# One instruction for both norms' variances and one for both biases, a shorter router, and undivided state slots only in two runs

## The chip, the cores and the metric

The kernel runs on one core of one Trainium2 chip. The metric is the device time of one execution in microseconds (us). TensorE (PE), VectorE (DVE), ScalarE (ACT), GpSimd (POOL) and SyncE (SP) each run their own instruction stream in order, and wait for each other through semaphores.

## The reference

One block of a network on 8 images of 192 channels and 16x16 = 256 positions (tokens):

```
x = x + conv(_ln_c(x))            # norm over channels; eps 1e-6
t = tokens(x)
t = t + ffn(_ln_t(t))             # norm over channels; eps 1e-5

conv(t): q, k = l2norm(silu(t Wq)), l2norm(silu(t Wk)); v = silu(t Wv); beta = sigmoid(t Wb)
         per head (12 heads of 16), over tokens t:
           u_t = beta_t (v_t - S^T k_t);  S = S + k_t u_t^T;  o_t = S^T q_t
         returns t + o Wo
ffn(x):  p = softmax(x router_w); top 2 of 8 experts, gates divided by their sum
         routed = sum_e gate_e * (silu(x w_gate_e) * (x w_up_e)) w_down_e
         shared = (silu(x ws_gate) * (x ws_up)) ws_down;  alpha = sigmoid(x sg_w + sg_b)
         returns alpha * shared + (1 - alpha) * routed
```

## The kernel before, in words

The 256 positions are cut into 16 chunks of 16 tokens; a chunk holds the 128 tokens of the 8 images and fills the 128 partitions. All engines go through steps c = -3 to 18 (`chunks`). In step c DVE runs the recurrence of chunk c, while the other engines and the gaps between DVE's recurrence instructions serve chunks that are earlier or later in the pipeline: `at(3, A_...)` is the first norm and the projections of chunk c+3, `at(-1, Fa_...)` the second norm and the router of chunk c-1, `Fb` the experts of chunks c-1 and c-2, `Fc` their output. The order in each step is written out by hand in each engine's `step`.

The recurrence of one chunk is 64 **slots** on DVE, four for each token: slot 4i multiplies the state by k (L1363, `Pr`), 4i+1 sums (L1365, `u`), 4i+2 forms k u^T (L1367, `bank`), 4i+3 adds it to the state (L1371, `SH`). Each needs the result of the one before. A slot is either **divided** (two instructions of half the heads, 96 elements each, so that one half works while the other's result lands) or **whole** (one instruction of 192), if its number is in `WHOLE`. `others(slot)` puts the small work of the other chunks behind a slot: `at(32, -1, Fa_var)` stands behind slot 32. A whole slot has to wait for its predecessor's result, and small work behind the predecessor fills that time.

Around the change:
- First norm (chunk c+3): `A_stats`, `A_mean` (L1091, L1095) make mean and variance, `A_var` (L1101) adds eps into `ve[:,0]`, POOL's `rsqrt` (L922) raises `ve` to -1/2 into `rs` for both norms at once, `A_bias` (L1108) makes `nmr1` = -mean*rstd, and ACT's `A_h`, `A_xh` use it. Second norm (chunk c-1): `Fa_stats`, `Fa_mean` (L1112, L1116), `Fa_var` (L1122), the same `rsqrt`, `Fa_bias` (L1128), then ACT's `Fa_h` (L662) writes `h2`, PE turns it, ACT's `Fa_hT` (L670) copies `hiT`, DVE's `Fa_split` (L1134) makes `loT`, and PE multiplies it by the router and the experts (L436 to L440).
- POOL, after `rsqrt`, does `hidden` 7, the products of state and q of half 0 of chunk c (L933), three `hidden`, the sums (L940, L957), and, after three small operations on k and q and two `hidden`, the same for half 1. DVE's `Fa_otok` (L1197) behind slot 23 of the next step waits for the second L957.
- ACT, after `Fa_h`, goes through some expert units, loads the table for exp and ln, does `A_inv` and `Fa_exp` (L678, L679: exp of the logits and of minus the shared gate's), loads the silu table, and copies `hidT` (`hidden` 2, L717). PE waits for that copy before `Fb_turn` 3 (L448), which stands ahead of `Fb_down` 2 (L463) and `fill(1, 0)` (L403). A `fill` broadcasts k for two tokens into PSUM, and slot 0 of the next step waits for `fill(1, 0)`.
- Router on DVE: `G_dif` makes the 64 differences of 8 logits, `G_eq` and `G_gt` compare them (equal ones count by order, table `lower`), `G_rank` sums to a rank, `G_sel` takes exp where rank < 2; `G_den`, `G_recip`, `G_rest`, `G_coef`, `G_gate` make the gates.

## Time and profile before

| | |
|---|---|
| time, median of 3 runs | 483.62 us (483.32 to 485.1) |
| the profiled execution's own time | 484.68 us |
| its span, first to last instruction | 482.9 us |
| granted clock of TensorE | 1.00 |
| DVE, PE, POOL, ACT busy | 86%, 86%, 85%, 72% of the span |
| DVE busy in each 25 us between 85 and 435 us | 24.3 to 24.9 us |

An engine's row in a timeline has its start, the time from its first start to its last end, and what it did; rows with x2 are two instructions of one form. The time from one row's start to the next row's start is what an instruction holds back its engine; this is less than its duration where two overlap.

### The profile page before, as it was taken

To read this page: it belongs to the slowest core of one execution; us is meant where nothing else is said; L and a number is where in the kernel's file an instruction comes from. 1 tells how busy PE (TensorE), PEld (TensorE's weight loads), DVE (VectorE), ACT (ScalarE), POOL (GpSimd) and SP (SyncE) were. 2 spreads that over 40 slices of the span, in tenths; PEclk is the share of its full clock that TensorE was granted. 3 is DMA by queue.
4 is the path that set the end of the run, shared out by engine and by line. 5 is a ranking of instruction groups with operands and counts; after the bars stand their busy time and mean duration, and the time that the engine had idled before them with its cause. 6 is when DMAs were issued, how large, how long until landed. Compare 5 with 4: busy or idle time off the path is not lost.

```text
span 482.9 us, 10362 instructions
## 1 busy us (share of the span) xinstructions
PE 416.3 (86%) x2400; PEld 384.6 (80%) x2400; DVE 415.3 (86%) x2258; ACT 347.4 (72%) x1003; POOL 410.8 (85%) x525
## 2 busy tenths in 40 slices
PE   1445265999999999999999999999999989899996
PEld 0323144898998999999999999999999979799895
DVE  4259899999999999999999999999999999996200
ACT  3699466587878687787878696969696847475862
POOL 4479798999999999999999999999999999986340
PEclk9999999999999999999999999999999999999999
DMA  6658372633233323323232233323232332300301
GB/s 163 164 131 176 92 194 76 124 88 117 78 83 80 88 65 96 76 87 87 71 87 83 87 87 83 93 80 92 72 99 71 84 90 76 94 5 1 115 2 16
DMA packets 43437, 42.91 MB, mean 89 GB/s; under 512 B 20144, under 2 KB 35184, under 8 KB 43376
## 3 DMA queue, kind: packets, MB, share of 16 engines
q1 hardware_dynamic: 42768, 42.05, 32.8%
q8 instruction: 19, 0.31, 0.3%
q14 instruction: 42, 0.34, 0.2%
q10 hardware_dynamic: 608, 0.21, 0.2%
HBM read 35.95 MB, written 6.29 MB: 87 GB/s over the span
## 4 chain that ended last, share of the span: by engine, by line
DVE 58%; PE 15%; POOL 9%; issue 8%; SPq 5%; DMA 3%; ACT 2%; POOLq 0%; ACTq 0%; DVEq 0%
DVE Pr L1363 13%; DVE bank L1367 13%; DVE u L1365 12%; DVE SH L1371 10%; PE bank L463 3%; POOL PQ L940 3%; POOL PQ L933 2%; POOL hid L978 2%; PE bank L436 1%; DMA k_scratch<-khl 1%; SPq L278 1%; PE bank L448 1%; PE bank L440 1%; PE bank L439 1%; PE bank L438 1%
## 5 line engine op out<-in xcount | busy, mean ns | idle before, releaser
L978 POOL TENSOR_TENSOR hid<-sg,ug 128x192 f32<-128x192 f32 x192 | 112.7, 606 | 22.0 <-ACT ug L707 18.8
L933 POOL TENSOR_TENSOR PQ<-SH,QB 128x768 f32<-128x768 f32 x62 | 112.6, 1838 | 0.7 <-DVE SH L1371 0.7
L706 ACT ACTIVATE sg<-bank 128x192 f32<-128x192 f32 x192 | 64.4, 336 | 61.1 <-PE bank L440 48.2
L940 POOL TENSOR_TENSOR PQ<-PQ 128x768 f32<-128x768 f32 (+2 forms) x93 | 102.9, 1106 | 6.1
L463 PE MATMUL bank<-Wd,hidT 128*128 128x192 f32 x576 | 106.6, 326 | 0.0
L1367 DVE TENSOR_TENSOR bank<-bank,u 128x96 f32<-128x96 f32 (+1 forms) x467 | 104.7, 266 | 0.6
L1363 DVE TENSOR_TENSOR Pr<-SH,bank 128x96 f32<-128x96 f32 (+1 forms) x437 | 101.3, 266 | 3.3 <-PE bank L403 1.3
L1365 DVE TENSOR_REDUCE u<-Pr 128x6 f32<-128x102 f32 (+1 forms) x437 | 102.6, 269 | 0.4
L1371 DVE TENSOR_TENSOR SH<-SH,bank 128x96 f32<-128x96 f32 (+1 forms) x467 | 102.2, 257 | 0.3
L463 PEld LDWEIGHTS bank<-Wd,hidT 128*128 128x128 f32 x576 | 94.5, 190 | 0.0
L436 PE MATMUL bank<-Whi,hiT 128*128 128x384 f32 (+1 forms) x192 | 73.1, 381 | 1.1 <-DVE loT L1134 1.1
L403 PE MATMUL bank<-KR,Sel 128*128 128x384 f32 x128 | 54.2, 426 | 18.7 <-DVE SH L1371 12.6
L440 PE MATMUL bank<-W,loT 128*128 128x384 f32 (+1 forms) x192 | 66.1, 344 | 0.0
L439 PE MATMUL bank<-W,hiT 128*128 128x384 f32 (+1 forms) x192 | 65.9, 343 | 0.0
L438 PE MATMUL bank<-Whi,loT 128*128 128x384 f32 (+1 forms) x192 | 65.9, 343 | 0.0
L437 PE MATMUL bank<-Wlo,hiT 128*128 128x384 f32 (+1 forms) x192 | 65.7, 342 | 0.0
L707 ACT ACTIVATE ug<-bank,gate 128x192 f32<-128x192 f32 x128 | 53.6, 419 | 0.0
L448 PE MATMUL bank<-ident,hid 128*128 128x128 f32 x288 | 45.6, 276 | 8.7 <-ACT hidT L717 8.0
L741 ACT ACT_TABLE_LOAD x38 | 48.8, 1283 | 0.7
L717 ACT ACTIVATE hidT<-bank 128x512 f32<-128x512 f32 (+1 forms) x80 | 45.7, 572 | 2.2 <-PE bank L448 2.0
L448 PEld LDWEIGHTS bank<-ident,hid 128*128 128x128 f32 x288 | 33.9, 141 | 14.7 <-issue 11.5
L403 PEld LDWEIGHTS bank<-KR,Sel 128*128 128x128 f32 x128 | 26.1, 206 | 23.1 <-DVE SH L1371 12.4
(141 smaller groups left out, 815.9 us busy)
## 6 DMA issues: line engine op xcount, KB each, us to landing
QB<-q_scratch SPq DMA_DIRECT2D x64, 384.0 KB
k_scratch<-khl SPq DMA_DIRECT2D x64, 48.0 KB, 1.7
KR<-k_scratch SPq DMA_DIRECT2D x32, 96.0 KB, 2.4
q_scratch<-qn SPq DMA_DIRECT2D x64, 24.0 KB, 1.6
...
```

What stands on the lines that cost most here:

```text
L403: mm(bKB[f % 2][:, 0:2 * BR * G], Sel[:, f].rearrange("p b x e -> p (b x e)"), KR[:, p, :], start=True, stop=True).then_inc(s_fill, 1)
L436: mm(to, hiT[:, p, 0:P], Whi0[:, w], start=True, stop=False)
L440: mm(to, loT[:, p, P:2 * P], W1[:, w], start=False, stop=True).then_inc(s_up, 1)
L448: last = tr(bHt[:, (k - lo) * P:(k - lo + 1) * P], hid[:, k % (KT // 2) * P:(k % (KT // 2) + 1) * P], ident[:, :])
L463: last = mm(bDn[:, 0:C], hidT[:, turn_half(g), k - lo, :], Wd[:, k, :], start=False, stop=(k == KT - 1))
L933: tt(PQ[:, at * BR * HP:(at + n) * BR * HP].rearrange("p (i b h) d -> p i b (h d)", i=n, b=BR), SH[:, lo:lo + n].rearrange("p i b h d -> p ...
L940: chained(tt(PQ[:, :, 0:w], PQ[:, :, 0:w], PQ[:, :, w:2 * w], ALU.add))
L978: tt(hid[:, r * H:(r + 1) * H], sg[:, m % RING], ug[:, m % RING], ALU.mult).then_inc(s_hid, 1)
L1363: v = each(slot, lambda lo, hi: count(tt(Pr[:, lo:hi, i, :, 0:D], prev[:, lo:hi], KB[:, lo:hi], ALU.mult)), Sb)
L1365: v = each(slot + 1, lambda lo, hi: count(nc.vector.tensor_reduce(u[:, i % 2, lo:hi], Pr[:, lo:hi, i], X, ALU.add, negate=True)), v)
L1367: v = each(slot + 2, lambda lo, hi: count(tt(KB[:, lo:hi], KB[:, lo:hi], u[:, i % 2, lo:hi].unsqueeze(3).to_broadcast([P, hi - lo, HP, D]) ...
L1371: ins = tt(SH[:, i, lo:hi], prev[:, lo:hi], KB[:, lo:hi], ALU.add)
```

## The change

`var_both` adds both eps values to both variances in one instruction behind slot 34 (before: two, behind slot 32), and `bias_both` makes both biases in one behind slot 38 (before: the second norm's behind slot 36, the first norm's behind 52). `Fa_mean` moves from slot 32 to 33, `A_vT` from 37 to 35. The router compares once, difference >= `above`: this table holds 0 where an equal logit counts and the smallest normal number where it doesn't. And the gates come from sel times 1/den times 1/(1 + exp(+sgate)), for which ACT does a third, one-column exp. `WHOLE` goes from 16 slots to 8: 31 to 34, 44, 48 to 50. In steps 13 to 15, where no first norm is left, `Fa_var` and `Fa_bias` stand at the new places.

```diff
-WHOLE = frozenset((9, 31, 32, 37, 44, 48, 49, 50, 51, 52, 53, 54, 55, 56, 57, 58))
+WHOLE = frozenset((31, 32, 33, 34, 44, 48, 49, 50))
+BOTH = NC - 4
+TINY = 1.1754944e-38
...
+        def variance2(q):
+            return (s_ve1, q + 5) if q < BOTH else (s_ve2, q - BOTH + 1)
+        def bias2(q):
+            return (s_nm1, q + 5) if q < BOTH else (s_nm2, q - BOTH + 1)
...
             def Fa_x1(q, p):
-                act.wait_ge(s_ve2, q + 1)
+                act.wait_ge(*variance2(q))
...
             def Fa_h(q, p):
-                act.wait_ge(s_nm2, q + 1)
+                act.wait_ge(*bias2(q))
...
                 f(prob[:, 0:E], bUp[0][:, 0:E], ACT.Exp, bias=negmax[:, 0:1])
-                f(prob[:, E:E + 1], bUp[0][:, E:E + 1], ACT.Exp, scale=-1.0, bias=neg_sgb[:, 0:1]).then_inc(s_pr, 1)
+                f(prob[:, E:E + 1], bUp[0][:, E:E + 1], ACT.Exp, scale=-1.0, bias=neg_sgb[:, 0:1])
+                f(prob[:, E + 1:E + 2], bUp[0][:, E:E + 1], ACT.Exp, bias=sgb[:, 0:1]).then_inc(s_pr, 1)
...
+            def var_both(q, p):
+                dve.wait_ge(*w["mv1"])
+                dve.wait_ge(*w["mv2"])
+                dve.wait_ge(s_rs, q + 4)
+                tt(ve[:, :], mv[:, :, 1], eps[:, :], ALU.add).then_inc(s_ve1, 1)
+
+            def bias_both(q, p):
+                dve.wait_ge(s_rs, q + 5)
+                dve.wait_ge(s_h, q + 4)
+                dve.wait_ge(s_xh, q + 4)
+                if later(q, 1):
+                    dve.wait_ge(s_h2, q)
+                nc.vector.scalar_tensor_tensor(out=nmr[:, :], in0=mv[:, :, 0], scalar=-1.0, in1=rs[:, :], op0=ALU.mult,
+                                               op1=ALU.mult).then_inc(s_nm1, 1)
...
-            def G_eq(q, p, slot):
-            def G_gt(q, p, slot):
+            def G_above(q, p, slot):
                 dve.wait_ge(s_nmx, q + 1)
+                w["above"] = count(tt(table(slot, 0), table(slot, 0), above[:, :, :], ALU.is_ge))
...
-                w["one"] = count(ts(den[:, 1:2], prob[:, E:E + 1], 1.0, None, ALU.add))
+                w["one"] = count(ts(den[:, 1:3], prob[:, E:E + 2], 1.0, None, ALU.add))
...
-            def G_rest(q, p, slot):
-            def G_coef(q, p, slot):
             def G_gate(q, p, slot):
-                dve.wait_ge(*w["co"])
-                tt(gate[:, p], scratch(slot, 0, 1).to_broadcast([P, E]), sel[:, :], ALU.mult).then_inc(s_gate, 1)
+                dve.wait_ge(*w["rden"])
+                ts(gate[:, p], sel[:, :], rden[:, p, 0:1], rden[:, p, 2:3], ALU.mult, ALU.mult).then_inc(s_gate, 1)
...
                         at(32, -1, Fa_stats)
-                        at(32, -1, Fa_mean)
-                        at(32, 3, A_var)
-                        at(32, -1, Fa_var)
-                        at(36, -1, Fa_bias)
-                        at(37, 1, A_vT)
+                        at(33, -1, Fa_mean)
+                        at(34, -1, var_both if c + 3 < NC else Fa_var)
+                        at(35, 1, A_vT)
+                        at(38, -1, bias_both if c + 3 < NC else Fa_bias)
...
-                        at(49, -1, G_eq, done)
-                        at(50, -1, G_gt, done)
-                        at(51, -1, G_rank, done)
-                        at(52, 3, A_bias)
+                        at(49, -1, G_above, done)
+                        at(50, -1, G_rank, done)
                         at(53, -1, G_sel, done)
                         at(54, -1, G_den, done)
-                        at(55, -1, G_recip, done)
-                        at(56, -1, G_rest, done)
-                        at(57, -1, G_coef, done)
+                        at(56, -1, G_recip, done)
                         at(58, -1, G_gate, done)
```

What DVE does before the change from slot 32 to slot 37 of a middle step (`st`, `mv` are the norms' statistics, `Pr`, `u`, `bank`, `SH` the slots; `128x6x16 x2` or `128x96 x2` is a divided slot):

```order
L1363 TENSOR_TENSOR Pr<-SH,bank 128x2x6x16
L1112 BN_STATS st<-bank 128x6
L1116 BN_AGGR mv<-st 128x2
L1101 TENSOR_SCALAR ve<-mv 128x1
L1122 TENSOR_SCALAR ve<-mv 128x1
L1365 TENSOR_REDUCE u<-Pr 128x6 x2
L1367 TENSOR_TENSOR bank<-bank,u 128x96 x2
L1371 TENSOR_TENSOR SH<-SH,bank 128x96 x2
L1363 TENSOR_TENSOR Pr<-SH,bank 128x6x16 x2
L1128 TENSOR_SCALAR nmr<-mv,rs 128x1
L1365 TENSOR_REDUCE u<-Pr 128x12
L1172 STREAM_TRANSPOSE vT<-vn 128x192
```

And after the change, from slot 32 to slot 38 of the same step:

```order
L1369 TENSOR_TENSOR Pr<-SH,bank 128x2x6x16
L1125 BN_STATS st<-bank 128x6
L1371 TENSOR_REDUCE u<-Pr 128x12
L1129 BN_AGGR mv<-st 128x2
L1373 TENSOR_TENSOR bank<-bank,u 128x2x96
L1147 TENSOR_TENSOR ve<-mv,eps 128x2
L1377 TENSOR_TENSOR SH<-SH,bank 128x96 x2
L1200 STREAM_TRANSPOSE vT<-vn 128x192
L1369 TENSOR_TENSOR Pr<-SH,bank 128x6x16 x2
L1371 TENSOR_REDUCE u<-Pr 128x6 x2
L1373 TENSOR_TENSOR bank<-bank,u 128x96 x2
L1155 SCALAR_TENSOR_TENSOR nmr<-mv,rs 128x2
```

Between the second norm's statistics and `ve` two whole slots now stand, and between `ve` and `nmr` four slots and the transpose, where there were four slots.

What DVE does after the change from slot 50 to slot 58 (before, each of these slots was whole, and had one or two small operations behind it):

```order
L1373 TENSOR_TENSOR bank<-bank,u 128x2x96
L1251 TENSOR_REDUCE bank<-bank 128x8
L1377 TENSOR_TENSOR SH<-SH,bank 128x96 x2
L1369 TENSOR_TENSOR Pr<-SH,bank 128x6x16 x2
L1371 TENSOR_REDUCE u<-Pr 128x6 x2
L1257 SCALAR_TENSOR_TENSOR sel<-bank,prob 128x8
L1259 TENSOR_SCALAR den<-prob 128x2
L1373 TENSOR_TENSOR bank<-bank,u 128x96 x2
L1263 TENSOR_REDUCE den<-sel 128x1
L1377 TENSOR_TENSOR SH<-SH,bank 128x96 x2
L1369 TENSOR_TENSOR Pr<-SH,bank 128x6x16 x2
L1269 RECIPROCAL rden<-den 128x3
```

Slots 51 to 58 are now divided, and the small operations stand further apart.

## Rows read from the trace of the kernel before

**Rows 1.** The page: busy time of the engines, and shares of the chain.
```profile
PE 416.3 (86%) x2400; PEld 384.6 (80%) x2400; DVE 415.3 (86%) x2258; ACT 347.4 (72%) x1003; POOL 410.8 (85%) x525
...
DVE 58%; PE 15%; POOL 9%; issue 8%; SPq 5%; DMA 3%; ACT 2%; POOLq 0%; ACTq 0%; DVEq 0%
```

**Rows 2.** Waits from 160 to 360 us: who waits for whom, total, times, longest.
```profile
PE bank L448 <- ACT hidT L717: 5.2, 8, 0.7
POOL rs L922 <- DVE ve L1122: 4.0, 8, 0.7
...
DVE ve L1122 <- DVE mv L1116: 0.3, 1, 0.3
```

**Rows 3.** Timeline of DVE, the instruction behind slot 23 in four steps.
```profile
92.14 0.38 DVE L1197 STREAM_TRANSPOSE otok<-oT 128x192 f32<-128x192 f32 x1
...
243.81 0.37 DVE L1197 STREAM_TRANSPOSE otok<-oT 128x192 f32<-128x192 f32 x1
...
269.01 0.37 DVE L1197 STREAM_TRANSPOSE otok<-oT 128x192 f32<-128x192 f32 x1
...
345.10 0.38 DVE L1197 STREAM_TRANSPOSE otok<-oT 128x192 f32<-128x192 f32 x1
```

**Rows 4.** Timeline of DVE, slots 32 to 38 of one step.
```profile
247.13 0.36 DVE L1363 TENSOR_TENSOR Pr<-SH,bank 128x192 f32<-128x192 f32 x1
247.40 0.36 DVE L1112 BATCH_NORM_STATS2 st<-bank 128x6 f32<-128x192 f32 x1
247.80 0.18 DVE L1116 BATCH_NORM_AGGREGATE mv<-st 128x2 f32<-128x6 f32 x1
...
248.01 0.15 DVE L1122 TENSOR_SCALAR ve<-mv 128x1 f32<-128x1 f32 x1
248.09 0.42 DVE L1365 TENSOR_REDUCE u<-Pr 128x6 f32<-128x102 f32 x2
...
249.40 0.21 DVE L1128 TENSOR_SCALAR nmr<-mv,rs 128x1 f32<-128x1 f32 x1
...
249.87 0.37 DVE L1172 STREAM_TRANSPOSE vT<-vn 128x192 f32<-128x192 f32 x1
250.16 0.40 DVE L1367 TENSOR_TENSOR bank<-bank,u 128x96 f32<-128x96 f32 x2
```

**Rows 5.** Timeline of DVE, slots 48 and 59 of the same step.
```profile
254.40 0.36 DVE L1363 TENSOR_TENSOR Pr<-SH,bank 128x192 f32<-128x192 f32 x1
254.67 0.23 DVE L1214 TENSOR_TENSOR bank<-bank,logit 128x64 f32<-128x64 f32 x1
...
258.84 0.42 DVE L1371 TENSOR_TENSOR SH<-SH,bank 128x96 f32<-128x96 f32 x2
```

**Rows 6.** Timeline of POOL, the same step.
```profile
248.43 0.70 POOL L922 TENSOR_TENSOR rs<-ve,neg_half 128x2 f32<-128x2 f32 x1 [0.40 <-DVE ve L1122]
...
268.51 0.37 POOL L957 TENSOR_TENSOR oT<-PQ 128x96 f32<-128x96 f32 x1
```

**Rows 7.** Timeline of ACT, the same step.
```profile
250.00 0.47 ACT L662 ACTIVATE h<-bank,nmr,rs 128x128 f32<-128x128 f32 x1
...
255.77 0.25 ACT L678 ACTIVATE prob<-bank,negmax 128x8 f32<-128x8 f32 x1
255.92 0.25 ACT L679 ACTIVATE prob<-bank,neg_sgb 128x1 f32<-128x1 f32 x1
...
257.48 0.60 ACT L717 ACTIVATE hidT<-bank 128x512 f32<-128x512 f32 x1
```

**Rows 8.** Timeline of PE, this step and the next.
```profile
258.23 0.63 PE L448 MATMUL bank<-ident,hid 128*128 128x128 f32 x4 [0.69 <-ACT hidT L717]
...
259.86 0.47 PE L403 MATMUL bank<-KR,Sel 128*128 128x384 f32 x1
...
283.45 0.63 PE L448 MATMUL bank<-ident,hid 128*128 128x128 f32 x4 [0.62 <-ACT hidT L717]
```

**Rows 9.** Timeline of DVE, slot 0 of the next step.
```profile
260.55 0.42 DVE L1363 TENSOR_TENSOR Pr<-SH,bank 128x96 f32<-128x96 f32 x2
```

More of the change, by code:

```diff
@@ L78, in build @@
         neg_half, eps6, one = sb("neg_half", [P, 2]), sb("eps6", [P, 1]), sb("one", [P, 1])
+        eps = sb("eps", [P, 2])
         sgb, neg_sgb = sb("sgb", [P, 1]), sb("neg_sgb", [P, 1])
-        lower = sb("lower", [P, E, E])
+        above = sb("above", [P, E, E])
         xs0, xs = sb("xs0", [C0, NB, T]), sb("xs1", [P, NB, T])
         xs1 = xs[C1:P]
-        st1, mv1 = sb("st1", [P, 6]), sb("mv1", [P, 2])
-        ve, rs, nmr1 = sb("ve", [P, 2]), sb("rs", [P, 2]), sb("nmr1", [P, 1])
+        st1, mv = sb("st1", [P, 6]), sb("mv", [P, 2, 2])
+        mv1, mv2 = mv[:, 0], mv[:, 1]
+        ve, rs, nmr = sb("ve", [P, 2]), sb("rs", [P, 2]), sb("nmr", [P, 2])
+        nmr1, nmr2 = nmr[:, 0:1], nmr[:, 1:2]
         rstd1, rstd2 = rs[:, 0:1], rs[:, 1:2]
@@ L863, in _ @@
             act.wait_ge(s_x[0], 32)
-            act.wait_ge(s_const, 4)
+            act.wait_ge(s_const, 6)
             chunks(step)
@@ L1063, in _ @@
                                pattern=[[-1, P]], channel_multiplier=1).then_inc(s_id, 1)
-            for t, val in ((neg_half, -0.5), (eps6, 1e-6), (one, 1.0), (ve, 1.0)):
+            for t, val in ((neg_half, -0.5), (eps6, 1e-6), (one, 1.0), (ve, 1.0), (eps[:, 0:1], 1e-6), (eps[:, 1:2], 1e-5)):
                 pool.memset(t[:, :], val).then_inc(s_const, 1)
-            pool.memset(lower[:, :, :], 1.0).then_inc(s_low, 1)
+            pool.memset(above[:, :, :], TINY).then_inc(s_low, 1)
             pool.wait_ge(s_low, 1)
-            pool.affine_select(out=lower[:, :, :], in_=lower[:, :, :], compare_op=ALU.is_gt, fill=0.0, base=0,
-                               pattern=[[1, E], [-1, E]], channel_multiplier=0).then_inc(s_low, 1)
+            pool.affine_select(out=above[:, :, :], in_=above[:, :, :], compare_op=ALU.is_ge, fill=0.0, base=0,
+                               pattern=[[-1, E], [1, E]], channel_multiplier=0).then_inc(s_low, 1)
             pool.memset(SH[:, T - 1], 0.0).then_inc(s_zero, 1)
@@ L1074, in _ @@
                 pool.memset(b, 0.0).then_inc(s_clear, 1)
-            pool.wait_ge(s_const, 4)
+            pool.wait_ge(s_const, 6)
             chunks(step)
@@ L1215, in G_dif @@
                    ALU.subtract).then_inc(s_nmx, 1)
-            def G_eq(q, p, slot):
+            def G_above(q, p, slot):
                 dve.wait_ge(s_nmx, q + 1)
-                w["eq"] = count(nc.vector.scalar_tensor_tensor(out=eq[:, :, :], in0=table(slot, 0), scalar=0.0,
-                                                               in1=lower[:, :, :], op0=ALU.is_equal, op1=ALU.mult))
-            def G_gt(q, p, slot):
-                dve.wait_ge(*w["eq"])
-                w["gt"] = count(nc.vector.scalar_tensor_tensor(out=table(slot, 0), in0=table(slot, 0), scalar=0.0,
-                                                               in1=eq[:, :, :], op0=ALU.is_gt, op1=ALU.add))
+                w["above"] = count(tt(table(slot, 0), table(slot, 0), above[:, :, :], ALU.is_ge))
             def G_rank(q, p, slot):
-                dve.wait_ge(*w["gt"])
+                dve.wait_ge(*w["above"])
                 w["rank"] = count(nc.vector.tensor_reduce(scratch(slot, E * E, E), table(slot, 0), X, ALU.add))
@@ L1247, in G_recip, with G_gate @@
                 w["rden"] = count(nc.vector.reciprocal(rden[:, p], den[:, :]))
-            def G_rest(q, p, slot):
+            def G_gate(q, p, slot):
                 dve.wait_ge(*w["rden"])
-                w["om"] = count(ts(coef[:, :], rden[:, p, 1:2], -1.0, 1.0, ALU.mult, ALU.add))
-            def G_coef(q, p, slot):
-                dve.wait_ge(*w["om"])
-                w["co"] = count(ts(scratch(slot, 0, 1), coef[:, :], rden[:, p, 0:1], None, ALU.mult))
-            def G_gate(q, p, slot):
-                dve.wait_ge(*w["co"])
-                tt(gate[:, p], scratch(slot, 0, 1).to_broadcast([P, E]), sel[:, :], ALU.mult).then_inc(s_gate, 1)
+                ts(gate[:, p], sel[:, :], rden[:, p, 0:1], rden[:, p, 2:3], ALU.mult, ALU.mult).then_inc(s_gate, 1)
             def negate_sgb():
@@ L1320, in others @@
                         at(48, -1, G_dif, done)
-                        at(49, -1, G_eq, done)
-                        at(50, -1, G_gt, done)
-                        at(51, -1, G_rank, done)
+                        at(49, -1, G_above, done)
+                        at(50, -1, G_rank, done)
                         at(53, -1, G_sel, done)
@@ L1326, in others @@
                         at(55, -1, G_recip, done)
-                        at(56, -1, G_rest, done)
-                        at(57, -1, G_coef, done)
                         at(58, -1, G_gate, done)
@@ L1377, in step @@
                         others(slot + 3)
-            dve.wait_ge(s_const, 4)
+            dve.wait_ge(s_const, 6)
             dve.wait_ge(s_low, 2)
```

13 lines of the change are left out of this document (6 added, 7 removed).

## The prediction

> **What bounds the kernel now.** The page says that four engines are busy for 72 to 86% of the span, and the chain that ended last lies on DVE for 58% [rows 1]. In the table of waits from 160 to 360 us, eight steps, the reader is to see that DVE waits once, for 0.3 us, while POOL waits for DVE's variance in each step and PE for ACT's `hidT` in each [rows 2]. So DVE sets the pace, by its own instructions: from `otok` to `otok` one undisturbed step takes 269.01 - 243.81 = 25.20 us, and over ten steps (92.14 to 345.10) the mean is 25.30, so that about 0.1 us a step goes to pauses like that 0.3 [rows 3]. A saving on DVE counts only as far as the loops through the other engines are shorter than 25.20. I therefore read the timelines for three loops.
>
> *The POOL loop.* `ve` is done at 248.01 + 0.15 = 248.16, `rsqrt` starts at 248.43 [rows 4, 6], and POOL works without a gap to the end of the second L957 at 268.88: 20.45 us [rows 6]. `otok` starts at 269.01, 0.13 later [rows 3]. A DVE instruction that really waits for a result starts 0.04 after it (247.40 + 0.36 to 247.80) [rows 4], so only 0.09 of this is slack. From `otok` (243.81) DVE needs 4.35 to `ve`. The loop's own length: 0.27 + 20.45 + 0.04 + 4.35 = 25.11.
>
> *The ACT-PE-DVE loop.* `nmr` ends at 249.61, ACT's `h` starts at 250.00 [rows 4, 7]: 0.39, so 0.35 of slack. ACT then goes on without a wait to `hidT` at 257.48, PE waits for it and resumes at 258.23, `fill(1, 0)` ends at 260.33, and slot 0 starts at 260.55: 0.22, so 0.18 of slack [rows 7, 8, 9]. Then DVE's slots 0 to 36 lead to the next `nmr`. Own length: 25.20 - 0.53 = 24.67.
>
> *The PE-ACT loop*, without DVE: PE resumes behind `hidT` at 258.23 and at 283.45, 25.22 apart [rows 8]. PE lacks nothing else in between, and ACT waits for PE's expert units, so this loop is full already.
>
> **The change, part by part.**
>
> *DVE's own time.* A divided slot costs 0.33: from slot 33 to `nmr` four of them take 249.40 - 248.09 = 1.31 [rows 4]. A whole one with a small operation behind it costs 0.40: eleven take 258.84 - 254.40 = 4.44 [rows 5]. Slots 48 to 58 are now three whole and eight divided ones, 1.21 + 2.64, and five small operations behind divided slots. Each costs about 0.09 there (such a one holds the queue for 248.09 - 248.01 = 0.08 [rows 4], the gate with two pointer operands perhaps 0.12): 0.45. Sum 4.30, saving 0.14. Around slot 32, from `st` to the start of slot 35: before 248.09 - 247.40 = 0.69 and two divided slots 0.66, together 1.35. After: `st` 0.27 (what a whole instruction holds the queue, 247.40 - 247.13), then two whole slots 0.80, with `mv` and `ve` inside: 1.07. Saving 0.28, of which about 0.05 is given back by the longer list of semaphores of `bias_both`. Slot 9 divided: 0.07 less. In all 0.4 to 0.44: DVE alone would need 24.8 us a step. The second comparison, the two gate operations and the two small norm operations are gone in this sum.
>
> *A page against this.* The Trainium skill, page "VectorE: DVE Perf Modes", section on the TRN2 errata, says that every instruction pays a fixed latency that shows between instructions, so many small tiles are worse than a large one, and gives (N + 151)/0.96 ns for fp32: 257 for 96 elements, 357 for 192. The durations agree (0.25 and 0.36), but by that rule a divided slot would cost 0.51, and here its halves overlap and it costs 0.33. It is kept as a rival below.
>
> *What is moved.* `ve` was ready 0.76 after `st` began (247.40 to 248.16). Now it is `st` 0.27, slot 33 whole until slot 34 may start 0.40, slot 34 until the small operation 0.27, and 0.15: 1.09. So **`ve` comes 0.33 later** against slot 30. From `ve`'s start to `nmr`'s it was 249.40 - 248.01 = 1.39. Now: the rest of slot 34 0.13, slot 35 0.33, `vT` 0.29 (249.87 to 250.16), slots 36 to 38 0.99: 1.74, or 0.35 more. So **`nmr` comes 0.68 later**. The first norm's bias comes much earlier than at slot 52, which serves nobody: ACT stands elsewhere in its order. Queued behind `rsqrt` on POOL are products, sums and then the L957 that `otok` waits for. Queued behind `Fa_h` on ACT are the units, `hiT`, the table loads, `hidT`.
>
> *What is added.* One more exp on ACT, between the second exp and the table load, in the gapless stretch from `h` to `hidT`. Bounds: 0, if something hid it, and its duration of 0.25. I take 0.15, from one exp's start to the next (255.77 to 255.92) [rows 7]. The Trainium skill, page "ScalarE: Activation LUTs", rules for kernel authors, budgets about 0.3 us for an activation. With that in place of 0.15, the two loops through ACT would be 0.15 longer.
>
> *The loops after.* POOL: 25.11 + 0.33 = **25.44**. ACT-PE-DVE: 24.67 + 0.68 + 0.15 - 0.07 = **25.43**. PE-ACT: 25.22 + 0.15 = **25.37**. All are longer than DVE's 24.8 and than the 25.20 of before. DVE has to stand still for about 0.65 us a step: at `otok` for POOL, at `loT` and slot 0 for ACT and PE. The two longest run side by side, so they don't add up.
>
> **Sum.** Steps 2 to 12, eleven of them, 25.44 - 25.20: +2.65. DVE's pauses of 0.1 a step now partly fall into its new idle time; between all and nothing of 11 x 0.1 I take half: -0.5. First step, where PE and ACT are still held up by the weights: the later `nmr` costs 0 to 0.7, taken 0.35. Steps 13 to 15 have no first norm, so shorter loops and more that DVE saves (bounds per step -0.4, its own saving, and +0.25, as above): taken 0. Behind the last step ACT's table, exp, table stands alone ahead of PE's wait, so the extra exp shows once more: +0.15. Together +2.65: 482.9 becomes a span of about 485.5, and the profiled execution's 484.68 about 487.3. That execution was 1.1 above the median of the three runs, and I put the difference on the median: 483.62 + 2.65 = 486.3.
>
> **Rivals.**
> 1. *Only the PE-ACT loop binds*, because the POOL loop and the ACT-PE-DVE loop have slack that I don't see (a shorter reaction of `rsqrt`, 0.27 now, with one semaphore less in its list). For it: the loops differ by 0.07 only. Against: both gaps are read directly. 11 x (25.37 - 25.30) + 0.15 = +0.9: 484.5.
> 2. *The exp is hidden and the moved operations too*: the floor is PE's present 25.22. 11 x (25.22 - 25.30), and up to 0.4 each in the last three steps: -2.1 at most, -1.2 in the middle: 482.4.
> 3. *DVE's saving comes through in full*: 14 steps of 0.4 and the pauses as before: 478. This needs POOL's 20.45 us to shrink by 0.65, which decides it: from 25.44 down to 25.30 nothing is won, and only below it the sign turns. For it: POOL's operations might run faster while DVE is idle. Against: POOL has no gap in that stretch.
> 4. *The waits hit in turn, not side by side*: `otok` late one time, then slot 0 late, with PE's and ACT's phases pushed by each; 0.5 to 0.6 a step instead of 0.25. 11 x 0.55, less what the pauses give: +5.8: 489.4.
> 5. *Each instruction pays in full*: halves that don't overlap, 0.50 instead of 0.36 for eight slots, 1.1 a step, +16 over 15 steps: 500. Forty-eight slots of every step are divided already and run at 0.33. This is the rule of the Trainium skill's VectorE page above; the trace does not agree with it.
>
> **How the numbers follow.** Forecast 0.50 (by itself 485.2 to 487.8), rival 1 0.19, rival 2 0.11, rival 3 0.09, rival 4 0.10, rival 5 0.01. A measurement here tells about 0.5%, 2.4 us, from no change: 481.2 to 486.0. The forecast's range lies across the upper edge, some three fifths above it: 0.30 slower, 0.20 same. With rivals 4 and 5 slower is 0.41. Rival 1 and most of rival 2 are same: 0.20 + 0.19 + 0.09 = 0.48. Rival 3 and the low end of 2 are faster: 0.09 + 0.02 = 0.11. Range: from 482.0, which leaves out rival 3 and a part of 2, to 488.8, which leaves out most of rival 4.
>
> **What the profile after would show.** Right: from `otok` to `otok` 25.4 to 25.5 in a middle step; DVE's waits with new lines of some tenths a step, `otok` for POOL's `oT`, `loT` for ACT's `hiT` or slot 0 for PE's L403 (now with new line numbers); POOL's idle time ahead of `rsqrt` about 0.65 where it was 0.40; ACT's `h` right behind `nmr`; DVE with 2,306 instructions (12 steps with 8 more and 5 fewer, three with 8 more and 3 fewer, the tail with 3 fewer), ACT with 1,019. Wrong: `otok` to `otok` of 24.8 with no wait on DVE (rival 3); 25.22 or 25.37 with `otok` not waiting (rivals 2, 1). The step most open to error is that a gap of 0.1 us, read at 0.01, decides between winning and losing.

## The result, and the profile after

The changed kernel takes 505.70 us (median of 4 runs, 505.62 to 506.04), the kernel before 483.51 us (4 runs, 483.32 to 485.1). The ratio is 1.0435 (95% interval 1.0411 to 1.046): 4.35% slower, some 22 us, where the prediction had 2.65. A few single executions further down came out far above the others of their kernel (553.98 us in e4, 504.24 in e9, 842.56 in e13); the ratios leave them out, the medians in the tables hold them.

The page of the kernel after: span, busy time, and the chain that ended last by engine and by line.
```profile
span 503.9 us, 10387 instructions
...
PE 416.7 (83%) x2400; PEld 382.8 (76%) x2400; DVE 430.9 (86%) x2306; ACT 351.8 (70%) x1019; POOL 413.1 (82%) x527
...
DVE 46%; PE 15%; ACT 14%; issue 8%; POOL 8%; SPq 5%; DMA 3%; ACTq 0%; POOLq 0%; DVEq 0%
DVE Pr L1369 10%; DVE u L1371 9%; DVE bank L1373 8%; DVE SH L1377 7%; ACT L754 5%; PE bank L475 4%; DVE nmr L1155 4%; POOL PQ L953 3%; PE bank L460 2%; ACT hidT L730 2%; POOL PQ L946 2%; POOL hid L991 2%; SPq L290 1%; DMA k_scratch<-khl 1%; ACT h L675 1%
```

DVE's share is what it was [rows 1], but its busy time has grown by 15.6 us, though the change was to relieve it. In the last line stands a name that did not appear in the prediction's sum: `nmr` L1155, the merged bias, with 4% of the span. Nothing else on DVE got longer by much; the groups of DVE instructions, each form apart (busy us, mean ns | idle time before), give the size:
```profile
L1155 DVE SCALAR_TENSOR_TENSOR nmr<-mv,rs 128x2 f32<-128x2 f32 x12 | 19.3, 1610 | 0.2 <-issue 0.2
...
L1274 DVE TENSOR_SCALAR gate<-sel,rden 128x8 f32<-128x8 f32 x16 | 5.1, 318 | 0.0
L1259 DVE TENSOR_SCALAR den<-prob 128x2 f32<-128x2 f32 x16 | 3.8, 239 | 0.0
...
L1147 DVE TENSOR_TENSOR ve<-mv,eps 128x2 f32<-128x2 f32 x12 | 1.8, 150 | 0.0
```

Twelve instructions on two elements a partition take 1.61 us each on average, where the old bias on one element took 0.21 [rows 4]. The merged variance beside it, as small, takes 0.15. The timelines of DVE and of POOL in one step show what the long one has for company (start, us from first start to last end):
```profile
260.79 0.42 DVE L1373 TENSOR_TENSOR bank<-bank,u 128x96 f32<-128x96 f32 x2
261.12 1.76 DVE L1155 SCALAR_TENSOR_TENSOR nmr<-mv,rs 128x2 f32<-128x2 f32 x1
262.81 0.41 DVE L1377 TENSOR_TENSOR SH<-SH,bank 128x96 f32<-128x96 f32 x2
```
```profile
259.82 0.70 POOL L935 TENSOR_TENSOR rs<-ve,neg_half 128x2 f32<-128x2 f32 x1 [0.87 <-DVE ve L1147]
260.49 0.60 POOL L991 TENSOR_TENSOR hid<-sg,ug 128x192 f32<-128x192 f32 x1
261.04 1.83 POOL L946 TENSOR_TENSOR PQ<-SH,QB 128x768 f32<-128x768 f32 x1
```

Two ends are to be compared here: `nmr` ends at 261.12 + 1.76 = 262.88, and POOL's product, which started 0.08 before it, at 261.04 + 1.83 = 262.87. DVE's next instruction starts 1.69 after `nmr` did; a small operation here holds it for about 0.1. The product reads two tensors in SBUF; so does `nmr` (`mv` and `rs`), and of all small operations that DVE has in a step, only this one and `ve` do. One view of this line over the whole execution (duration ns min/median/max, then who waited for it):
```profile
L1155 DVE SCALAR_TENSOR_TENSOR nmr<-mv,rs x12: 288/1758/1762, 72.3 to 369.8; 128x2 f32<-128x2 f32 x12
...
  ACT h L674: 19.9, 12
```

The waits from 160 to 360 us, seven steps (total, times, longest), answer to [rows 2]:
```profile
ACT h L674 <- DVE nmr L1155: 11.3, 7, 1.6
...
PE bank L367 <- ACT h L675: 10.1, 7, 1.4
...
ACT oc L663 <- PE bank L363: 9.2, 7, 1.3
PE bank L460 <- ACT hidT L730: 7.5, 8, 0.9
...
POOL rs L935 <- DVE ve L1147: 6.1, 7, 0.9
...
DVE loT L1162 <- ACT hiT L682: 3.2, 7, 0.5
```

ACT waits 1.6 us a step for the bias, PE for ACT's `h` behind it, and the wait `DVE loT`, which the prediction named, is there with 0.46 a step. The step follows from the twelve starts of `otok` over which both norms run, eleven steps apart (first and last start stand in the row behind the three durations); it answers to [rows 3]:
```profile
L1225 DVE STREAM_TRANSPOSE otok<-oT x12: 367/371/373, 92.3 to 390.3; 128x192 f32<-128x192 f32 x12
```
(390.3 - 92.3)/11 = 27.09 us a step; in the kernel before it is 25.30 [rows 3]. 11 x 1.79 = 19.7 of the span's 21.0 us are in these eleven steps.

Three theories stood to be told apart. **Port:** a DVE instruction with two tensor inputs in SBUF waits until POOL's running instruction ends. **Form:** the merged instruction is slow in itself, by its operation, its two elements or its four semaphores. **Places:** the later places of variance and bias and the third exp make the longer step, as my prediction had it, only more so.

### The profile page after: what moved, and what is told of

It is laid out like the page before. It is cut to its first block, busy times and chain, and to the rows that moved or that the text cites. A ratio compares the mean times of both kernels' runs of the same rounds, so it can differ in the third digit from the quotient of the medians.

```text
span 503.9 us, 10387 instructions
## 1 busy us (share of the span) xinstructions
PE 416.7 (83%) x2400; PEld 382.8 (76%) x2400; DVE 430.9 (86%) x2306; ACT 351.8 (70%) x1019; POOL 413.1 (82%) x527
## 4 chain that ended last, share of the span: by engine, by line
DVE 46%; PE 15%; ACT 14%; issue 8%; POOL 8%; SPq 5%; DMA 3%; ACTq 0%; POOLq 0%; DVEq 0%
DVE Pr L1369 10%; DVE u L1371 9%; DVE bank L1373 8%; DVE SH L1377 7%; ACT L754 5%; PE bank L475 4%; DVE nmr L1155 4%; POOL PQ L953 3%; PE bank L460 2%; ACT hidT L730 2%; POOL PQ L946 2%; POOL hid L991 2%; SPq L290 1%; DMA k_scratch<-khl 1%; ACT h L675 1%
## 5 line engine op out<-in xcount | busy, mean ns | idle before, releaser
L991 POOL TENSOR_TENSOR hid<-sg,ug 128x192 f32<-128x192 f32 x192 | 113.9, 612 | 35.6 <-ACT ug L720 29.0
L953 POOL TENSOR_TENSOR PQ<-PQ 128x768 f32<-128x768 f32 (+2 forms) x93 | 103.1, 1109 | 6.1
L1369 DVE TENSOR_TENSOR Pr<-SH,bank 128x96 f32<-128x96 f32 (+1 forms) x467 | 102.5, 257 | 3.1 <-PE bank L415 1.1
L1371 DVE TENSOR_REDUCE u<-Pr 128x6 f32<-128x102 f32 (+1 forms) x482 | 104.2, 255 | 0.1
L1377 DVE TENSOR_TENSOR SH<-SH,bank 128x96 f32<-128x96 f32 (+1 forms) x497 | 103.7, 248 | 0.3
```

Source lines behind the costliest of these rows:

```text
L953: chained(tt(PQ[:, :, 0:w], PQ[:, :, 0:w], PQ[:, :, w:2 * w], ALU.add))
L991: tt(hid[:, r * H:(r + 1) * H], sg[:, m % RING], ug[:, m % RING], ALU.mult).then_inc(s_hid, 1)
L1369: v = each(slot, lambda lo, hi: count(tt(Pr[:, lo:hi, i, :, 0:D], prev[:, lo:hi], KB[:, lo:hi], ALU.mult)), Sb)
L1371: v = each(slot + 1, lambda lo, hi: count(nc.vector.tensor_reduce(u[:, i % 2, lo:hi], Pr[:, lo:hi, i], X, ALU.add, negate=True)), v)
L1377: ins = tt(SH[:, i, lo:hi], prev[:, lo:hi], KB[:, lo:hi], ALU.add)
```

## The experiments

The kernels of one group ran on the same chip beside the kernel before, and ratios are to that (its medians: 484.13, 484.41, 484.56 and 484.12 us in the four groups). A mean step is worked out as above, over the same eleven steps, from the one execution of each kernel that was profiled.

### First group: is it the port, the form or the places?

**e1_two_biases**
```diff
-                nc.vector.scalar_tensor_tensor(out=nmr[:, :], in0=mv[:, :, 0], scalar=-1.0, in1=rs[:, :], op0=ALU.mult,
-                                               op1=ALU.mult).then_inc(s_nm1, 1)
+                ts(nmr2[:, :], mv2[:, 0:1], rstd2, -1.0, ALU.mult, ALU.mult)
+                ts(nmr1[:, :], mv1[:, 0:1], rstd1, -1.0, ALU.mult, ALU.mult).then_inc(s_nm1, 1)
```


> The changed kernel with its one merged bias instruction (two tensor inputs in SBUF) written as the two old instructions of one tensor input and a pointer each, at the same slot 38 and behind the same waits; all else as changed. Port theory (a DVE instruction with two tensor inputs in SBUF waits until GpSimd's running instruction ends): each bias takes 0.21 us and holds DVE about 0.12, so DVE gets back 1.69 - 0.24 = 1.45 us a step; the step falls from 27.10 to between 25.2 and 25.5, and the time from 505.7 to 482-488. Rival, the later places of variance and bias and the third exp make the step: the step stays near 27.1 and the time near 505.

**e2_slot37**
```diff
-                        at(38, -1, bias_both if c + 3 < NC else Fa_bias)
+                        at(37, -1, bias_both if c + 3 < NC else Fa_bias)
```


> The changed kernel with the merged bias instruction unchanged in form, but one slot earlier (37 for 38). Port theory: it starts near the end of GpSimd's 0.6 us instruction hid, before the product of 1.83 us; it takes 0.3 to 0.4 us, holds DVE about 0.3, and the time is 486-490. Rival, the instruction of this form and shape is slow in itself, or its list of semaphores is: it still takes 1.6 to 1.8 us and the time stays at 503-506.

**e4_lone_two_sbuf** (the kernel before, with)
```diff
...
+            def extra(q, p):
+                nc.vector.scalar_tensor_tensor(out=junk[:, :], in0=neg_half[:, :], scalar=-1.0, in1=neg_half[:, :], op0=ALU.mult,
+                                               op1=ALU.mult)
...
+                        if c + 3 < NC:
+                            at(38, -1, extra)
```


> The kernel before with one instruction added in 12 steps, at slot 38: a scalar_tensor_tensor of 2 elements a partition whose two tensor inputs are one constant in SBUF and which nobody waits for. It has no semaphore. In this kernel GpSimd's first product (1.84 us) ends about 1.0 us after slot 38. Port theory: each takes 0.9 to 1.1 us and holds DVE nearly as long, +10 to +12 us, time 493 to 496. Rival, the form is slow by itself: 1.6 to 1.8 us each, about 502. Rival, it waited in the changed kernel for its data or its list of semaphores: 0.16 us each, 484 to 485.

**e5_lone_psum**: the same with `in1=bKB[0][:, 0:2]`, which is in PSUM.

> The kernel before with the same lone instruction at the same slot in 12 steps, but with its second tensor input in PSUM. Port theory: 0.16 us each and the time 483.5 to 485.5. Rival, the form is slow in itself: as with both inputs in SBUF, 1 us or more each and 493 or more.

Measured:

| | ratio (95%) | median us | mean step | the instruction in question |
|---|---|---|---|---|
| e1 | 1.0138 (1.0109 to 1.0167) | 490.83 | 25.72 | 0.20 us each |
| e2 | 1.0103 (1.0069 to 1.0136) | 488.82 | 25.43 | 0.31 us |
| e4 | 1.0231 (1.0192 to 1.0269) | 495.91 | 26.18 | 1.04 us |
| e5 | 0.9997 (0.9979 to 1.0014) | 483.98 | 25.29 | 0.14 us |

The same merged instruction with the same operands and semaphores is short one slot earlier. DVE and POOL in e2_slot37:
```profile
250.75 0.30 DVE L1155 SCALAR_TENSOR_TENSOR nmr<-mv,rs 128x2 f32<-128x2 f32 x1
```
```profile
250.44 0.60 POOL L991 TENSOR_TENSOR hid<-sg,ug 128x192 f32<-128x192 f32 x1
251.00 1.83 POOL L946 TENSOR_TENSOR PQ<-SH,QB 128x768 f32<-128x768 f32 x1
```
It ends at 251.05, with `hid` at 251.04, not with the product that follows. And an instruction that nobody waits for, on a constant, behind no semaphore, put into the kernel before, lasts until POOL's product there ends, to 0.02 us (255.83 + 1.04 = 256.87; 255.01 + 1.84 = 256.85); e4_lone_two_sbuf, DVE and POOL:
```profile
255.83 1.04 DVE L1132 SCALAR_TENSOR_TENSOR junk<-neg_half 128x2 f32<-128x2 f32 x1
256.79 0.41 DVE L1378 TENSOR_TENSOR SH<-SH,bank 128x96 f32<-128x96 f32 x2
```
```profile
255.01 1.84 POOL L934 TENSOR_TENSOR PQ<-SH,QB 128x768 f32<-128x768 f32 x1
```
With one of its inputs in PSUM it is an ordinary small operation (view of the line in e5_lone_psum, ns min/median/max):
```profile
L1132 DVE SCALAR_TENSOR_TENSOR junk<-neg_half,bank x12: 141/144/148, 71.9 to 350.6; 128x2 f32<-128x2 f32 x12
```
So the port theory stands, and form and semaphores are out: with two inputs in SBUF the same form takes 0.31, 1.04 and 1.76 us, each time what POOL leaves of its own instruction, and with one of them in PSUM 0.14. In e4 each of them costs 0.96 us of DVE's queue, and its step is 26.18 - 25.29 = 0.89 longer than e5's; the ratio, from three executions, gives 0.0231 x 484 = 11.2 us (9.3 to 13.0) for the twelve: where DVE sets the pace, such a wait is paid nearly in full. Places are out as the main cause: e1 keeps them all, and with it 4.35% have become 1.38%.

The Trainium skill says this, page "SBUF — State Buffer", section "Who interferes with whom": a VectorE instruction with two SBUF inputs contends with a GpSimd instruction that reads SBUF, since its second input comes through a read interface that the two share, and the one that comes second is blocked until the other's instruction ends. The trace agrees: POOL's instructions in these rows all read SBUF, and DVE's end 0.01 to 0.02 us after them.

The kernel before had a row for it already, the other way round. At its end DVE takes over one product with two inputs in SBUF, and POOL's `hid`, which needs 1.15 for two, takes 3.06 (before, DVE and POOL):
```profile
436.51 1.76 DVE L1180 TENSOR_TENSOR PQ<-SH,QB 128x1536 f32<-128x1536 f32 x1
```
```profile
435.10 1.15 POOL L978 TENSOR_TENSOR hid<-sg,ug 128x192 f32<-128x192 f32 x2
436.93 3.06 POOL L978 TENSOR_TENSOR hid<-sg,ug 128x192 f32<-128x192 f32 x2 [0.69 <-ACT ug L707]
```
The first of the two takes 1.79 and ends 0.45 after DVE's product (436.51 + 1.76 = 438.27).

What e1 and e2 did not bring back, 1.0 to 1.4%, is more than the 0.55% of the prediction, and e1 missed the 482 to 488 expected of it. In both, the router's new forms have become long in places (view of the two lines in e2_slot37; in the kernel after their medians are 159 and 282 ns):
```profile
L1259 DVE TENSOR_SCALAR den<-prob x16: 160/487/916, 79.7 to 457.2; 128x2 f32<-128x2 f32 x16
L1274 DVE TENSOR_SCALAR gate<-sel,rden x16: 293/381/530, 81.8 to 457.8; 128x8 f32<-128x8 f32 x16
```
What they cost in e2 is open: its step of 25.43 is that of e9 below (25.44), where they are short. In e1, ACT's `h` waits for the second of the two biases and starts 6.69 after `otok`, against 6.49 in e3 below (251.59 - 244.90, 252.55 - 246.06), and its usual step is 25.65 for e3's 25.49; one step of 26.86, in which `den` takes 0.85 and `gate` 0.62, comes on top.

### Second group: the same without any such wait

**e3_psum_means**: means and variances are written to PSUM, so that the merged bias has one input there.
```diff
...
+            mvp = scratch(33, 96, 4).rearrange("p (n k) -> p n k", n=2)
+            def means_both(q, p):
+                dve.wait_ge(*w["st1"])
+                nc.vector.bn_aggr(mvp[:, 0], st1[:, :]).then_inc(s_chain, 1)
...
+                w["mvp"] = count(nc.vector.bn_aggr(mvp[:, 1], st2[:, :]))
...
-                nc.vector.scalar_tensor_tensor(out=nmr[:, :], in0=mv[:, :, 0], scalar=-1.0, in1=rs[:, :], op0=ALU.mult,
+                nc.vector.scalar_tensor_tensor(out=nmr[:, :], in0=mvp[:, :, 0], scalar=-1.0, in1=rs[:, :], op0=ALU.mult,
...
-                        at(31, 3, A_mean)
...
-                        at(33, -1, Fa_mean)
+                        at(33, -1, means_both if c + 3 < NC else Fa_mean)
```


> The changed kernel with the means and variances of both norms written to PSUM (both of them at slot 33), so that the merged bias instruction, of the same form and size, at the same slot 38 and behind the same semaphores, reads one tensor in PSUM and one in SBUF. Port theory: it takes 0.15 to 0.2 us where it took 1.76, the step falls from 27.10 to about 25.45, and the time is 485-489. Rival, merging the two biases is slow in any form: 1.6 us or more each and 503-506.

**e7_no_port**: e3, with the router's selection, denominators and gate input in PSUM too, and
```diff
...
-                w["one"] = count(ts(den[:, 1:3], prob[:, E:E + 2], 1.0, None, ALU.add))
+                w["one"] = count(ts(scratch(53, 81, 2), prob[:, E:E + 2], 1.0, None, ALU.add))
...
-                ts(gate[:, p], sel[:, :], rden[:, p, 0:1], rden[:, p, 2:3], ALU.mult, ALU.mult).then_inc(s_gate, 1)
+                ts(gate[:, p], scratch(53, 72, 8), rden[:, p, 0:1], rden[:, p, 2:3], ALU.mult, ALU.mult).then_inc(s_gate, 1)
...
-                        at(56, -1, G_recip, done)
-                        at(58, -1, G_gate, done)
+                        at(54, -1, G_recip, done)
+                        at(54, -1, G_gate, done)
```


> As the last one, and the router's selection and denominators in PSUM too (reciprocal and gate moved to slot 54, where that bank is still free), so that no small instruction of VectorE reads two tensors in SBUF or runs from SBUF to SBUF over an even number of elements, but the two variances' sum. Port theory: den takes 0.16 and gate 0.28 us in every step, none ends 25 ns after an instruction of GpSimd; DVE gets back the 0.07 to 0.35 us a step that both waited; step 25.1 to 25.4, time 481-487. Rival, the loop over GpSimd and the late bias sets the step, as my prediction had it: it stays at 25.4 to 25.45 however little DVE does, time 486-488, with DVE idle for the difference.

**e8_norms_old**: the changed kernel with the old norms.
```diff
...
-                        at(33, -1, Fa_mean)
-                        at(34, -1, var_both if c + 3 < NC else Fa_var)
-                        at(35, 1, A_vT)
-                        at(38, -1, bias_both if c + 3 < NC else Fa_bias)
+                        at(32, -1, Fa_mean)
+                        at(32, 3, A_var)
+                        at(32, -1, Fa_var)
+                        at(36, -1, Fa_bias)
+                        at(37, 1, A_vT)
...
+                        at(52, 3, A_bias)
```


> The router's and the undivided slots' part of the change alone: variances and biases as in the kernel before, four instructions at the old slots. DVE's own time is some 0.2 us a step under that of before, less what den (two elements) and gate (SBUF to SBUF) wait for GpSimd, 0 to 0.45 us. Port theory: the time is that of before within 1%, and den or gate end 25 ns after an instruction of GpSimd wherever they are long. Rival, the third exp or the router's new order costs by itself: over 488 with den and gate short.

**e9_no_port_37**: e7 with `bias_both` at slot 37.

> As e7_no_port, with the merged bias one slot earlier (37). If the late bias held loT (VectorE idle 0.4 us a step before it with the bias at 38 in two instructions, 0.0 with it at 37), the step is that of VectorE's own work, 24.8 to 25.1, and the time 478-483, under the kernel before. Rival, the loops over GpSimd's rsqrt and the expert stream set it: 25.4, 486-488.

| | ratio (95%) | median us | mean step | `nmr` | `den` min/median/max ns | `gate` |
|---|---|---|---|---|---|---|
| e3 | 1.0073 (1.005 to 1.0096) | 488.53 | 25.49 | 0.15 us | 158/306/596 | median 383 |
| e7 | 1.0066 (1.0042 to 1.009) | 488.21 | 25.53 | 0.15 | 151/152/155 | 284/285/286 |
| e8 | 1.007 (1.0047 to 1.0093) | 488.49 | 25.59 | 0.21 | 157/160/939 | 282/284/633 |
| e9 | 1.0067 (1.0039 to 1.0094) | 488.43 | 25.44 | 0.15 | as e7 | as e7 |

e3 is the changed kernel but for where its means lie. Its `nmr`, over all twelve:
```profile
L1163 DVE SCALAR_TENSOR_TENSOR nmr<-bank,rs x12: 148/150/160, 73.3 to 354.6; 128x2 f32<-128x2 f32 x12
```
From 1.0435 to 1.0073: 3.6 of the 4.35% were the second SBUF input of twelve instructions of two elements, 17.5 us. Their busy time gives the same: 19.3 in the kernel after, less 12 x 0.15.

e8 shows the second, smaller form of the same thing. DVE in a step of 26.44 us, and POOL beside it:
```profile
182.52 0.89 DVE L1259 TENSOR_SCALAR den<-prob 128x2 f32<-128x2 f32 x1
183.32 0.42 DVE L1375 TENSOR_TENSOR bank<-bank,u 128x96 f32<-128x96 f32 x2
...
185.13 0.63 DVE L1274 TENSOR_SCALAR gate<-sel,rden 128x8 f32<-128x8 f32 x1
```
```profile
180.52 2.87 POOL L953 TENSOR_TENSOR PQ<-PQ 128x768 f32<-128x768 f32 x2
...
185.14 0.59 POOL L991 TENSOR_TENSOR hid<-sg,ug 128x192 f32<-128x192 f32 x1
```
`den` has one tensor input, two elements, from SBUF to SBUF; it ends at 183.41, POOL's L953 at 183.39. `gate` ends at 185.76, POOL's `hid` at 185.73. Where they meet nothing they take 0.16 and 0.28. With one element, in the kernel before, `den` was never long (142/143/144 ns over its 16), and with their input or output in PSUM (e7) both are constant to 4 ns. Most steps of e8 without such a meeting take 25.25 us, the three with both 26.44. That is 3 x 1.19 = 3.6 us, about the whole of its 0.7%. The Trainium skill, page "VectorE: DVE Perf Modes", section "Mode 2×_2P — use both read ports for one tensor", has a rule for it: an fp32 tensor_scalar from SBUF to SBUF whose outermost dimension is even in source and destination reads through both interfaces, and PSUM on either side excludes that. The runs agree.

e7 and e9 are then the changed kernel with every such wait gone, and they test the sum that I had made. In e7, as in e3, with the bias at the predicted slot 38, DVE pauses only ahead of `loT`, which starts 0.87 after the slot before it where an unpaused one has 0.33; `otok` doesn't wait. In e9 a step takes 25.44, and DVE stands idle at just the two places named: at `otok`, and at `loT` (waits of DVE and POOL from 160 to 360 us, e9_no_port_37):
```profile
POOL rs L935 <- DVE ve L1146: 5.2, 8, 0.7
...
DVE loT L1170 <- ACT hiT L682: 1.4, 7, 0.2
```
and DVE's and POOL's rows at `otok`: it starts 0.53 after the divided slot before it, which holds the queue for 0.32 or 0.33, and 0.03 after POOL's `oT` ended (244.74 + 0.37 = 245.11).
```profile
244.61 0.41 DVE L1384 TENSOR_TENSOR SH<-SH,bank 128x96 f32<-128x96 f32 x2
245.14 0.38 DVE L1233 STREAM_TRANSPOSE otok<-oT 128x192 f32<-128x192 f32 x1
```
```profile
241.17 3.49 POOL L953 TENSOR_TENSOR PQ<-PQ 128x768 f32<-128x768 f32 x3
244.74 0.37 POOL L970 TENSOR_TENSOR oT<-PQ 128x96 f32<-128x96 f32 x1
```
That is the POOL loop of the prediction, at its length of 25.44. By starts, DVE pauses 0.2 at `otok` and 0.27 ahead of `loT` (0.60 for 0.33), a little more than the view of waits has.

### Third group: the places, the exp, the merging alone

**e10_early**: e7 with the old places (the variances, which wait for both means, at 33).
```diff
                         at(32, -1, Fa_stats)
-                        at(33, -1, means_both if c + 3 < NC else Fa_mean)
-                        at(34, -1, var_both if c + 3 < NC else Fa_var)
-                        at(35, 1, A_vT)
-                        at(38, -1, bias_both if c + 3 < NC else Fa_bias)
+                        at(32, -1, means_both if c + 3 < NC else Fa_mean)
+                        at(33, -1, var_both if c + 3 < NC else Fa_var)
+                        at(36, -1, bias_both if c + 3 < NC else Fa_bias)
+                        at(37, 1, A_vT)
```


> As e7_no_port, but with means, variances and bias at the slots of the kernel before (32, 33 and 36 for 33, 34 and 38). With no wait for GpSimd left, the step was 25.50 us with the bias at 38 and 25.43 at 37, and VectorE stood idle 0.2 us before loT and 0.22 us in slot 32. Loop theory (the late variance and the late bias of my prediction hold the step at 25.4): with both back the step falls to VectorE's own work, 24.9 to 25.2, and the time to 479-484. Rival, the third exp and the expert stream set it: 25.4 and 486-489.

**e12_late_places**: the kernel before with
```diff
-                        at(32, -1, Fa_mean)
-                        at(32, 3, A_var)
-                        at(32, -1, Fa_var)
-                        at(36, -1, Fa_bias)
-                        at(37, 1, A_vT)
+                        at(33, -1, Fa_mean)
+                        at(34, 3, A_var)
+                        at(34, -1, Fa_var)
+                        at(35, 1, A_vT)
+                        at(38, -1, Fa_bias)
```


> The kernel before with its old instructions, but the norms' mean, variances, transpose vT and bias at the places of the changed kernel (33, 34, 35 and 38 for 32, 32, 37 and 36). Loop theory: 25.40 to 25.45 a step for 25.18, that is 486-487. Rival, VectorE alone sets the pace of before and the places are free: 25.2 and 483-485.

**e6_extra_exp**: the kernel before with
```diff
...
-                f(prob[:, E:E + 1], bUp[0][:, E:E + 1], ACT.Exp, scale=-1.0, bias=neg_sgb[:, 0:1]).then_inc(s_pr, 1)
+                f(prob[:, E:E + 1], bUp[0][:, E:E + 1], ACT.Exp, scale=-1.0, bias=neg_sgb[:, 0:1])
+                f(prob[:, E + 1:E + 2], bUp[0][:, E:E + 1], ACT.Exp, bias=sgb[:, 0:1]).then_inc(s_pr, 1)
```


> The kernel before with the third exp added on ScalarE behind the second, its result read by nobody. My prediction's loop over VectorE and the expert stream: +0.15 us of VectorE waiting before sel, of which all is on the path: 25.33 a step, 485.5-486.5. Rival, it is hidden: VectorE comes to sel later than ScalarE ends, 483.5-484.5.

**e11_norms_psum**: the kernel before with `means_both`, `var_both` and `bias_both` as in e10 and
```diff
-WHOLE = frozenset((9, 31, 32, 37, 44, 48, 49, 50, 51, 52, 53, 54, 55, 56, 57, 58))
+WHOLE = frozenset((9, 32, 37, 44, 48, 49, 50, 51, 53, 54, 55, 56, 57, 58))
```


> The kernel before with only the norms merged, means and variances in PSUM, at the old places (statistics and means 32, variances 33, bias 36), router and exps as before, slots 31 and 52 divided. If the merging itself is worth what it takes from VectorE (four small instructions fewer by two, two slots divided), 0.2 to 0.3 us a step: 24.9 to 25.05 and 479-482. Rival, another loop holds the step where it is: 25.18 and 483-485, with VectorE idle for the difference.

| | ratio (95%) | median us | mean step |
|---|---|---|---|
| e10 | 1.0 (0.9984 to 1.0016) | 484.7 | 25.35 |
| e12 | 1.0169 (1.0145 to 1.0194) | 492.65 | 25.84 |
| e6 | 1.0021 (1.0004 to 1.0038) | 485.45 | 25.35 |
| e11 | 1.0066 (1.004 to 1.0093) | 487.88 | 25.44 |

e10 against e7: the places alone, with all else of the change, are worth 0.66%, give or take 0.3. With them back and no wait for POOL, the change costs and brings nothing: 1.0, where both expectations were off (I had 479 to 484 or 486 to 489). e12 shows the same from the other side, and harder than I had expected: 0.53 us a step and not 0.25, DVE waiting for `hiT`:
```profile
DVE loT L1134 <- ACT hiT L670: 2.8, 6, 0.5
```
(Waits of DVE from 160 to 320 us.) With the old instructions and the old `WHOLE`, the second norm's bias starts 6.55 us after `otok` there, in e3 6.25, and the undisturbed step is longer by about as much, 25.76 for 25.49.

The third exp costs 0.2%, 1.0 us. The expectation for e6 had 2, from a full 0.15 in each step; the prediction's rival 1 had 0.9, since only what exceeds DVE's pace counts. PE shows it plainly (e6_extra_exp, two resumptions behind `hidT`, one step apart):
```profile
235.24 0.63 PE L448 MATMUL bank<-ident,hid 128*128 128x128 f32 x4 [0.82 <-ACT hidT L718]
...
260.59 0.63 PE L448 MATMUL bank<-ident,hid 128*128 128x128 f32 x4 [0.83 <-ACT hidT L718]
```
From 159 to 337 us all seven such intervals are 25.35 to 25.38, while DVE's steps go from 25.18 to 25.85. In the kernel before, five of eight are 25.22 or 25.23 [rows 8], the other three 25.36 to 25.38. So with the third exp the loop between PE and ACT is about 25.36 long, as the prediction had it (25.37).

e11 is a miss: it has less work on DVE than the kernel before and the old places, and is 0.7% slower. No wait of DVE on another engine over 0.3 us shows between 160 and 320. Part of the cause is in its `WHOLE`: slots 31 and 52, which are divided and stand ahead of a whole slot with nothing behind them, hold DVE for 0.54 and 0.51 in each step, where the whole slot with its small operation held it for 0.47 and 0.38. That is 0.20 a step more, as much as the whole edit was to save at the least. One step of 27.98 near the end is in no other trace; the profiled execution is the slowest of e11's ten (490.97, the fastest 485.59), and I have no cause for that step.

### Fourth group: can the saving on DVE be had?

**e13_between**: e7 with
```diff
-                        at(34, -1, var_both if c + 3 < NC else Fa_var)
+                        at(33, -1, var_both if c + 3 < NC else Fa_var)
                         at(35, 1, A_vT)
-                        at(38, -1, bias_both if c + 3 < NC else Fa_bias)
+                        at(36, -1, bias_both if c + 3 < NC else Fa_bias)
```


> As e9_no_port_37, but with the variances' sum at slot 33 right behind the means and the bias at 36. Loop theory: the loops over GpSimd's rsqrt and over ScalarE's h shorten by the slot, 0.3 us, to 25.1; VectorE's own work is 24.9 to 25.1; step 25.0 to 25.2 and the time 480-483.5, under the kernel before or level. Rival, saving and lateness are one thing (what the late places hide on VectorE is what comes back as stalls when they are early): 25.25 to 25.4 and 484-486.

**e14_between_den53**: e13 with `at(53, -1, G_den, done)` for 54.

> As e13_between, with den's sum at slot 53 in place of 54, so that two and not three instructions that wait for each other stand in slot 54. If VectorE sets the step there, 0.05 to 0.1 us a step less than e13_between, about 1 us in all; if another loop does, the same time as e13_between.

Both 1.0018 (1.0001 to 1.0036, and 0.9999 to 1.0037), 485.08 and 485.47 us, mean steps of 25.35 and 25.34: neither version is below the kernel before, as e13's rival had it. e14 tests nothing more, since its edit took nothing from DVE: from `G_dif` to slot 55 both need 3.01 us (253.97 to 256.98, 254.23 to 257.24). Three kernels with the new router and the third exp (e10, e13, e14) stand at 25.35, next to the 25.36 of the loop between PE and ACT, and in e10 and e13 PE's resumptions are 25.33 to 25.38 apart too. DVE waits there, but too shortly for the view of waits: ahead of `loT` for ACT's `hiT`, 0.54 where 0.33 is usual (e10_early):
```profile
250.94 0.41 DVE L1384 TENSOR_TENSOR SH<-SH,bank 128x96 f32<-128x96 f32 x2
251.48 0.42 DVE L1170 TENSOR_TENSOR loT<-bank,hiT 128x256 fp32r<-128x256 f32 x1
```
So these rows speak for the loop between PE and ACT as what holds them; no run made it shorter in these kernels, which would show it.

## Why the prediction was wrong, point by point

**The step that failed** is the price of `bias_both`: "about 0.05 is given back by the longer list of semaphores", with the instruction itself taken at what a small operation holds the queue, 0.08 to 0.09. It holds it for 1.69 us, because it waits, inside its own duration, for the end of POOL's product; the prediction had no such wait. I had priced all small operations of the change by rows of small operations, and did not look at what their operands were: every small operation in a step of the kernel before has at most one tensor input in SBUF, the rest being PSUM or a scalar, so there was no row of that size for the new one. It was bounded from neither side, though the trace had what gives the upper bound: POOL's product of 1.84 us stands across slot 38 in the middle steps, as e4 in the old kernel shows, and POOL's `hid` beside DVE's product at the end of the kernel had shown the wait itself. In time: 11 x 1.60 (27.09 against 25.49 in e3) are 17.6 us. By the ratios, e3 against the kernel after, it is 3.6 of the 4.35%, 17.5 us.

**Right, once that wait is gone.** Without it the changed kernel is 0.7% slower than before (e3, e7, e9: 1.0066 to 1.0073), the prediction said 0.55% (2.65 us). `ve` comes 1.09 after the second norm's statistics, as worked out (in the trace after, from 258.47 to 259.56), and `nmr` starts 1.71 after `ve` does, for 1.74. POOL's idle time before `rsqrt` is 0.65 in e9, as named. The step of the POOL loop, 25.44, is e9's; at the predicted places (e3, e7) it is 25.49 to 25.50 and DVE pauses at `loT` alone, so there the ACT-PE-DVE loop holds, for which I had 25.43. PE-ACT is 25.36 in e6 for 25.37. Instruction counts, 2,306 and 1,019, are as said. DVE's own time comes out too: in the trace after, the step of 27.08 from 254.79, less 1.61 for `nmr`, 0.54 ahead of `loT` and 0.12 at slot 0, leaves 24.8, and from `st` to the start of slot 35 it takes the 1.07 that I had.

**Partly right.** From `logit` to the end of slot 58 it is 4.66 us in the kernel before and 4.55 in the one after, a saving of 0.11 for my 0.14. But e8, with the new router and the first norm's bias at slot 52 again, takes 4.68: the saving is the bias that left, and the shorter router gives nothing. Places: 0.66% between e10 and e7, 3.2 us with some 1.5 either way, for the 2.65 that they and the exp were given together.

**The rivals.** None of the five was this one, and none had a wait between DVE and POOL other than by semaphore. Rival 5 (500 us) came nearest in time and is wrong in mechanism: divided slots in the trace after still hold the queue for 0.33 (260.79 to 261.12). Rival 1, 484.5 by the loop of PE and ACT alone, is what e10 measured with its 484.7, and by the loop that it names, as far as the rows above go, but not for the kernel that was predicted.
